# One iteration of a pipelined Mamba-2 block with a mixture of experts: the same operations in another order on every engine

## The reference

```python
# attention half (a Mamba-2 block), for each sequence
qkv = layernorm(x) @ W_in.T;  q = rope(qkv[:, :, 0])
zxbcdt = rmsnorm(q, norm_pre_w) @ W_zxbcdt.T              # z, (x, B, C), dt
xBC = silu(conv4(xBC) + conv_b);  dt = softplus(dt + dt_bias)
y = ssd(x_ssm, dt, -exp(A_log), B, C) + D * x_ssm         # scan over the sequence in chunks
out = rmsnorm(y * silu(z), norm_gated_w) @ W_out.T + q
x = x + layernorm(out)
# feed-forward half, for each token
h = layernorm(x)
shared = (silu(h @ sg.T) * (h @ su.T)) @ sd.T             # 512 hidden
scores = sigmoid(h @ router_w.T)                          # 16 experts in 4 groups
# the best 2 groups, the best 4 experts in them, their scores normalised: combine (token, expert)
routed = sum_e (silu(h @ gate_w[e]) * (h @ up_w[e]) * combine[:, e]) @ down_w[e]   # 16 x 64 hidden
x = x + layernorm(shared + routed)
```

## Time and profile before

| | us |
|---|---|
| median of 3 runs | 3214.55 (3213.54 to 3217.93) |
| the profiled execution | 3218.34 |
| its span | 3216.4 |
| TensorE, VectorE, ScalarE, POOL busy | 3116.9, 2393.1, 1931.1, 2033.7 |
| from one loop iteration to the next | 96.40 |

### The profile page before, as it was taken

How to read it: one execution, slowest core, us unless ns; L and a number is a source line. 1 busy time by engine, 2 the same in 40 slices (tenths; PEclk the granted TensorE clock), 3 DMA queues, 4 the chain that set the end, 5 groups by cost and what they waited for, 6 DMA issues and landing times.

```text
span 3216.4 us, 62379 instructions
## 1 busy us (share of the span) xinstructions
PE 3116.9 (97%) x19648; PEld 2723.4 (85%) x19648; DVE 2393.1 (74%) x5104; ACT 1931.1 (60%) x4146; POOL 2033.7 (63%) x2311
## 2 busy tenths in 40 slices
...
GB/s 109 40 70 80 66 59 74 73 76 79 66 60 75 72 77 78 66 60 74 72 78 76 66 63 72 72 79 76 66 65 71 71 79 76 66 67 69 71 80 40
DMA packets 143434, 227.33 MB, mean 71 GB/s; under 512 B 18977, under 2 KB 88353, under 8 KB 143393
## 3 DMA queue, kind: packets, MB, share of 16 engines
...
...
## 4 chain that ended last, share of the span: by engine, by line
PE 94%; POOL 1%; DMA 0%; DVE 0%; ACT 0%; issue 0%; SPq 0%; POOLq 0%; ACTq 0%; DVEq 0%
PE fpb L1325 33%; PE apb L1325 19%; PE acc L1504 17%; PE apb L1450 7%; PE apb L1334 4%; PE ppb L1325 3%; PE apb L1435 3%; PE apb L1442 2%; PE ppb L1344 2%; PE apb L1422 1%; PE fpb L1374 1%; PE fpb L1344 1%; PE fpb L1376 1%; PE fpb L1483 0%; PE apb L1395 0%; POOL hid L541 0%
## 5 line engine op out<-in xcount | busy, mean ns | idle before, releaser
L546 POOL TENSOR_TENSOR hidL<-hid,hidH 128x512 fp32r<-128x512 f32 x384 | 545.8, 1421 | 216.8 <-ACT hidH L801 207.5
L1015 DVE SCALAR_TENSOR_TENSOR xc<-apb,cw,xc 128x511 f32<-128x511 f32 (+2 forms) x576 | 427.8, 748 | 67.8 <-ACT xc L714 39.5
L1504 PE MATMUL acc<-WDH,hidH 128*128 128x256 f32 x1536 | 458.2, 298 | 6.2 <-POOLq L548 5.9
L801 ACT CAST hidH<-hid 128x512 fp32r<-128x512 f32 x384 | 236.1, 615 | 353.6 <-POOL hid L541 288.7
L1504 PE MATMUL acc<-WDH,hidL 128*128 128x256 f32 x1536 | 432.0, 281 | 0.0
L1504 PE MATMUL acc<-WDL,hidH 128*128 128x256 f32 x1536 | 431.5, 281 | 0.0
L541 POOL TENSOR_TENSOR hid<-hid,cb 128x512 f32<-128x512 f32 x256 | 347.2, 1356 | 81.8 <-DVEq L1136 43.7
L1134 DVE TENSOR_TENSOR hid<-hid,fpb 128x512 f32<-128x512 f32 x384 | 261.1, 680 | 135.4 <-PE fpb L1325 125.2
L1325 PE MATMUL fpb<-fTh,UH 128*128 128x512 f32 x768 | 336.1, 438 | 0.8 <-ACTq L793 0.8
L732 ACT ACTIVATE seg<-seg,acs 128x128 f32<-128x128 f32 x1024 | 313.8, 389 | 10.2 <-ACT cb L782 5.9
L1325 PE MATMUL fpb<-fTh,GH 128*128 128x512 f32 x768 | 317.5, 413 | 0.0
...
## 6 DMA issues: line engine op xcount, KB each, us to landing
seg<-acs_row SPq DMA_DIRECT2D x128, 512.0 KB, 4.2
cb<-c_row SPq DMA_DIRECT2D x512, 128.0 KB, 2.9
...
```

What stands on the lines that cost most here:

```text
L546: own.do(G.tensor_tensor(hidL[:, j % 2, :], hid[:, j % 2, :], hidH[:, j % 2, :].bitcast(fp32), ALU.subtract))
L801: A.copy(hidH[:, j % 2, :], hid[:, j % 2, :]).then_inc(sem["hidden_high"], 1)
L1015: ins = V.scalar_tensor_tensor(xc[:, b, s:], src[:, 0:T - s], cw[:, b, TAPS - 1 - s:TAPS - s], xc[:, b, s:], ALU.mult, ALU.add)
L1504: ins = nc.tensor.matmul(dst, l[:, w, tk], r[:, j, :], start=j == 0 and t % 2 == 0 and n == 0, stop=j == HB - 1 and n == 2, skip_group_che ...
```

## The change

Only orders change: the slots of A and F, FREED to match, and the five functions `iteration`. No operation is added or taken away on TensorE, VectorE, POOL and SyncE. On ScalarE `exp_table` and `silu_table` stand more often in the list. The diff of the five orders, without their indentation; the slots and FREED ("..." at its head) follow from them:

```diff
...
@@ -434,15 +434,14 @@  # SyncE
             def iteration(i, p, a, f, g):
 if f: save_x1(i - 1)
 if a: decay_store(); decay_rows(0); decay_rows(1)
+if p: load_next(i + 1)
 if f: combine_store(); combine_rows(0)
-if p: load_next(i + 1)
+if a: decay_rows(2)
 if f: combine_rows(1)
-if a: decay_rows(2); decay_rows(3)
+if a: decay_rows(3)
 if f: combine_rows(2)
-if a: keep_q()
-if f: combine_rows(3)
-if a: load_x(i)
-if f: combine_rows(4); combine_rows(5); combine_rows(6); combine_rows(7)
+if a: keep_q(); load_x(i)
+if f: combine_rows(3); combine_rows(4); combine_rows(5); combine_rows(6); combine_rows(7)
 if p: settle_p()
 if a: settle_a()
 if f: settle_f()
@@ -587,21 +586,20 @@  # POOL
 
             def iteration(i, p, a, f, g):
 if g: norm_out()
-if f: rest(0)
+if f: rest(0); rest(1)
+if a: mask(0)
 if g: add_result(i - 2)
-if f: rest(1); rest(2)
-if a: mask(0)
-if f: hold_shift()
-if a: mask(1)
+if f: rest(2)
 if g: result_stored()
-if a: decayed(0); decayed(1)
-if f: rest(3); combine(4)
-if a: gated(0)
-if f: combine(5); rest(4)
+if a: decayed(0); mask(1)
+if f: rest(3)
+if a: decayed(1); gated(0)
+if f: combine(4)
 if a: mask(2); decayed(2)
-if f: rest(5)
+if f: rest(4); combine(5)
 if p: norm_px()
-if a: mask(3); gated(1)
+if f: rest(5); hold_shift()
+if a: gated(1); mask(3)
 if f: combine(6)
 if a: gated(2)
 if f: rest(6)
@@ -609,16 +607,15 @@  # POOL, further down
 if f: combine(7)
 if p: rope_sum(0)
 if f: rest(7)
-if a: norm_mixed(0)
+if p: root_q(0)
 if f: combine(8)
-if a: gated(3)
+if a: norm_mixed(0); gated(3)
 if f: rest(8)
-if p: root_q(0)
+if p: rope_sum(1)
+if a: root_y(1)
 if f: combine(9)
-if a: root_y(1)
-if p: rope_sum(1)
+if p: root_q(1)
 if f: rest(9)
-if p: root_q(1)
 if a: norm_mixed(1); norm_x1(0)
 if f: combine(10)
 if a: norm_x1(1)
@@ -825,69 +822,63 @@  # ScalarE
 for names in freed.values():
     names.clear()
 if w: silu_table()
-if a: conv_first(4); silu_z(0, 0); silu_z(1, 0)
+if a: conv_first(4); silu_z(0, 0); silu_z(0, 1)
 if f: f_high(0); f_high(1)
-if a: conv_first(5); conv_silu(4); silu_z(2, 0); conv_silu(5); exp_table(); softplus()
-if a: conv_first(0); silu_table(); silu_z(3, 0)
+if a: conv_silu(4); silu_z(1, 0); silu_z(2, 0); exp_table(); softplus(); conv_first(5)
+if a: silu_table(); silu_z(3, 0); conv_first(0)
 if f: gate(0)
+if a: conv_silu(5)
+if f: gate(1)
 if a: conv_first(1); conv_silu(0)
-if f: score_tanh()
-if a: conv_first(2)
-if f: round_hidden(0)
-if a: conv_silu(1)
-if f: gate(1)
-if a: silu_z(0, 1); conv_silu(2)
-if f: gate(2)
 if g: final_norm()
-if a: conv_first(3)
-if f: round_hidden(1)
-if a: silu_z(1, 1)
+if a: conv_silu(1); conv_first(2)
+if f: round_hidden(0); round_hidden(1)
+if a: conv_first(3); conv_silu(2)
+if f: gate(2); score_tanh()
+if a: evac_B(); conv_silu(3); evac_CB(); exp_table(); decays()
 if f: round_hidden(2)
-if a: evac_B(); conv_silu(3)
-if f: gate(3); gate(4)
-if a: evac_CB(); silu_z(2, 1); exp_table(); decays()
-if f: evac_cT()
 if a: exp_seg(0)
 if w: split_high(3)
-if f: round_hidden(3)
-if a: exp_seg(1)
+if a: silu_table(); silu_z(1, 1); silu_z(2, 1)
+if f: gate(3)
+if a: silu_z(3, 1)
 if w: split_high(4)
+if f: gate(4); evac_cT(); round_hidden(3)
+if a: exp_table(); exp_seg(1)
+if w: split_high(5)
 if a: silu_table()
-if f: gate(5)
-if a: silu_z(3, 1)
-if w: split_high(5)
-if f: round_hidden(4); round_hidden(5); gate(6)
+if f: gate(5); round_hidden(4)
 if a: exp_table(); exp_seg(2)
 if w: split_high(6)
+if a: silu_table()
+if f: gate(6); round_hidden(5)
 if a: evac_y(0)
 if w: split_high(7)
-if p: norm_x(0)
-if a: exp_seg(3)
+if a: square_y(0)
 if w: split_high(8)
-if a: silu_table()
 if f: gate(7)
-if a: square_y(0)
+if p: norm_x(0); norm_x(1)
+if a: exp_table(); exp_seg(3)
 if w: split_high(9)
 if p: evac_xT(0)
+if f: round_hidden(6)
 if a: evac_y(1)
 if w: split_high(10)
-if f: round_hidden(6)
 if a: square_y(1)
 if w: split_high(11)
-if f: round_hidden(7); gate(8)
-if p: norm_x(1); square_q(0)
+if a: silu_table()
+if f: gate(8); round_hidden(7)
+if p: square_q(0); evac_xT(1)
 if a: evac_y(2)
-if p: evac_xT(1)
+if f: round_hidden(8)
 if a: square_y(2)
-if f: round_hidden(8); gate(9)
+if f: gate(9)
 if a: evac_y(3); square_y(3)
-if f: round_hidden(9)
 if p: square_q(1)
-if f: gate(10)
+if f: gate(10); round_hidden(9)
 if p: h_high(0); h_high(1)
-if f: gate(11)
 if a: norm_x1(0)
-if f: round_hidden(10)
+if f: gate(11); round_hidden(10)
 if a: norm_x1(1)
 if f: round_hidden(11)
 if p: settle_p()
@@ -1208,35 +1199,37 @@  # VectorE
             def iteration(p, a, f, g, w=False):
 for names in freed.values():
     names.clear()
-if a: dt_bias_add(0); dt_bias_add(1); conv(4)
+if a: dt_bias_add(0); conv(4); dt_bias_add(1)
 if f: f_low(0)
 if a: dt_bias_add(2)
 if f: f_low(1)
-if a: conv(5)
-if f: route_logits()
 if a: dt_bias_add(3)
 if g: final_moments()
-if a: dt_finish(); conv(0)
+if a: conv(5); dt_finish(); conv(0); conv(1)
 if f: up(0)
-if a: conv(1); conv(2)
-if f: route_scores()
 if a: evac_acs()
-if f: up(1); route_groups(); up(2)
+if f: up(1)
+if a: conv(2)
+if f: route_logits()
 if a: conv(3)
-if f: route_experts(); up(3)
-if a: times_dt(0); times_dt(1); decay_CB(0)
+if f: route_scores(); up(2); route_groups()
+if a: times_dt(0)
+if f: route_experts()
+if a: decay_CB(0)
+if f: up(3)
+if a: times_dt(1); chunk_y(0); new_state(0); decay_CB(1)
+if w: split_low(3)
 if f: up(4)
-if a: new_state(0); chunk_y(0)
+if a: times_dt(2)
 if f: up(5)
-if a: state_part(1); decay_CB(1)
-if w: split_low(3)
-if a: new_state(1); times_dt(2); chunk_y(1)
+if a: state_part(1)
+if p: moments_px()
+if a: new_state(1); chunk_y(1)
 if w: split_low(4)
-if p: moments_px()
+if a: decay_CB(2); state_part(2); y_low(0); new_state(2)
+if w: split_low(5)
 if f: up(6)
-if a: state_part(2); decay_CB(2); y_low(0); new_state(2)
-if w: split_low(5)
-if a: chunk_y(2); times_dt(3); decay_CB(3)
+if a: times_dt(3); chunk_y(2); decay_CB(3)
 if p: x_low(0)
 if a: y_low(1)
 if f: up(7)
@@ -1245,17 +1238,16 @@  # VectorE, further down
 if w: split_low(6); split_low(7)
 if a: state_part(3)
 if f: up(8)
-if a: chunk_y(3); y_low(2)
 if p: x_low(1)
-if a: add_x(0)
+if a: chunk_y(3); y_low(2); add_x(0)
 if w: split_low(8); split_low(9)
+if p: rope(1); norm_q(0)
+if a: y_low(3)
 if f: up(9)
-if a: y_low(3)
-if p: rope(1); norm_q(0)
 if a: mixed_out(1)
 if w: split_low(10)
+if p: norm_q(1); h_low(0)
 if f: up(10)
-if p: norm_q(1); h_low(0)
 if a: add_x(1)
 if w: split_low(11)
 if p: h_low(1)
@@ -1524,80 +1516,90 @@  # TensorE
 open_.update(n for n, (who, part, _, _) in SEM.items()
              if who == "PE" and {"p": p, "a": a, "f": f, "g": g}[part])
 if w: weights_split(KD + 1)
-if a: project_z(0, 0); project_z(1, 0)
+if a: project_z(0, 0)
 if f: ffn_by_channel(0)
+if a: project_z(0, 1)
+if f: ffn_by_channel(1)
 if a: project_x(4)
-if f: ffn_by_channel(1)
+if f: settled("ffn_in_ready")
 if g: down(10)
-if f: settled("ffn_in_ready")
-if a: project_z(2, 0); project_x(5)
+if a: project_z(1, 0); project_z(2, 0)
 if g: down(11); settled("last_split")
-if f: logits(0); logits(1)
-if a: project_z(3, 0); project_x(0)
+if a: project_z(3, 0); project_x(5)
 if f: gate(0)
+if a: project_x(0)
+if f: gate(1)
 if a: project_x(1)
 if f: up(0)
-if a: project_x(2)
-if f: gate(1); up(1)
-if a: project_z(0, 1); cumulate()
+if a: cumulate()
+if f: up(1)
+if a: settled("ad_ready"); project_x(2)
+if f: logits(0)
+if a: project_x(3)
+if f: logits(1)
+if a: CB()
 if f: gate(2)
-if a: settled("ad_ready"); project_z(1, 1); project_x(3)
+if a: B_by_token()
 if f: up(2); gate(3); down(0); settled("acc_free")
-if a: B_by_token(); project_z(2, 1)
-if f: gate(4)
-if a: CB(); x_by_token(0)
-if f: up(3); down(1)
-if a: x_by_token(1)
-if f: combine_by_expert(); down(2); settled("c_ready"); up(4); gate(5)
-if a: state(0); project_z(3, 1); diagonal(0)
+if a: x_by_token(0); project_z(1, 1)
+if f: down(1)
+if a: project_z(2, 1)
+if f: down(2)
+if a: project_z(3, 1)
+if f: gate(4); up(3)
+if a: state(0)
+if f: combine_by_expert()
+if a: x_by_token(1); diagonal(0)
+if f: up(4); settled("c_ready"); gate(5)
+if a: x_by_token(2)
+if f: down(3)
+if a: from_state(1); state(1)
 if f: up(5)
-if a: from_state(1); state(1)
-if f: down(3)
-if a: x_by_token(2)
+if a: diagonal(1)
 if f: gate(6)
-if a: diagonal(1); from_state(2)
-if f: up(6); down(4)
 if a: y_by_channel(0)
-if f: gate(7)
-if a: state(2)
-if f: up(7)
-if a: settled("xdec_ready"); diagonal(2); x_by_token(3)
+if f: gate(7); down(4)
+if a: from_state(2); state(2)
+if f: up(6)
+if a: settled("xdec_ready")
 if f: down(5)
+if a: x_by_token(3); diagonal(2)
+if f: gate(8)
 if a: settled("a_out_ACT")
 if w: weights_split(KD + 2)
 if a: project_out(0)
 if p: x_by_channel(0)
 if a: y_by_channel(1)
-if f: gate(8)
+if f: up(7)
 if a: from_state(3)
 if p: project_q(0)
 if a: project_out(1)
 if f: down(6); up(8)
-if a: y_by_channel(2); diagonal(3)
-if f: down(7)
-if a: settled("m_ready")
+if a: y_by_channel(2)
 if p: x_by_channel(1)
+if a: diagonal(3)
 if f: gate(9)
 if p: settled("xn_ready")
```

(39 more changed lines are left out.)

14 lines of the change are left out of this document (7 added, 7 removed).

## The result

The changed kernel takes 3242.32 us (median, 3240.67 to 3243.28), the kernel before beside it 3216.24: a ratio of 1.008, with 1.0062 to 1.0097 as its 95% interval. I had forecast 3212. It is slower by more than I could put down to a measurement.

The account below looks back on a forecast made before the run. TensorE was taken to bound the kernel. From the profiled 3218.34 us, -1.5 (boundary), +1 (ramp) and -2 (tail) gave 3215.8, and the median lying 3.8 lower gave 3212, no measurable change; range 3200 to 3240.

Parts of the forecast that it names:

- What bounds the kernel: Whole kernel: TensorE, busy 96.36 of a steady iteration's 96.40 us; only its lost time there can be won.
- the prize of the boundary: Between up(11) and the next project_z(0, 0): a wait of 0.28 us per iteration, 8.4 us or 0.26% over 30 boundaries.
- The boundary: From up(11) into the next iteration: h_low(1) early, the wait goes, new lateness takes 0.23; 96.35 us, a 1.5 us gain.
- the exchange with down(10): After the boundary: the 0.28 us won is mostly lost again, 0.19 at down(10) and 0.04 at the half z behind.
- The step that failed: Start of the iteration: project_z(0, 0) to down(10) keeps its length of 3.71 us in the new order.
- ScalarE: ScalarE's queue: ten table loads an iteration for six, 5.1 us more work, 65 of 96.4 us, covered; priced at 0.
- cover "in sum": ScalarE: four added loads cost nothing because its share only goes from 59.8 to 65 us of 96.4.
- Routing: Mid-iteration, route_experts to diagonal(0) and up(5): producers stay in time, slack 0.9 to 1.9 and 1.0 us; priced at 0.
- the slack of up(5): Mid-iteration: up(4) frees the bank at 47.8 and up(5) needs it at 48.8, slack 1.0 us.
- Rival B: Mid-iteration wait, route_experts through decay_CB and exp_seg(1) to up(5): 0.7 us an iteration, period 97.1, 3234 us; chance 0.27.
- Ramp (+1): Iteration 0: added loads nearly cancel with earlier CB and decays; +1 us, between -3 and +5.1.
- tail (-2): Last feed-forward: rests go ahead of the next combine, combine(11) starts about 2 us earlier; -2 us, between 0 and -3.

Follow-up runs that it names:

- before_hpair: Kernel before, TensorE's h_by_channel(0) ahead of up(10) and h_by_channel(1) ahead of gate(11), VectorE's h_low(0) and norm_q(1) ahead of up(10): 3218.08 us, ratio 0.9998.
- before_ffn1: Kernel before with one edit on TensorE, ffn_by_channel(1) ahead of project_x(4): 3237.44 us, ratio 1.0067.
- ffn_dve: Changed kernel with ffn_by_channel(1) back behind project_x(4) on TensorE and norm_q(0) behind y_low(3) and up(9) on VectorE: 3221.80 us, ratio 1.0012.
- dve_y: Changed kernel with norm_q(0) on VectorE moved behind y_low(3) but still ahead of up(9): 3229.60 us, ratio 1.0035.
- ffn_back: Changed kernel with ffn_by_channel(1) on TensorE moved back behind project_x(4): 3231.89 us, ratio 1.0042.
- dve_q: Changed kernel with norm_q(0) on VectorE moved behind y_low(3) and up(9): 3226.41 us, ratio 1.0027.
- no_loads: Changed kernel without its four added ScalarE table loads: 3240.70 us, ratio 1.007.
- before_loads: Kernel before with four more table loads an iteration, a pair behind exp_seg(0) and a pair behind exp_seg(2): 3285.68 us, ratio 1.0221.
- ffn_dve_loads: Changed kernel, ffn_by_channel(1) behind project_x(4), norm_q(0) behind y_low(3) and up(9), two more table loads in front of exp_seg(1): 3279.24 us, ratio 1.0198.
- before_h1: Kernel before with one edit on TensorE, h_by_channel(1) ahead of gate(11): 3237.75 us, ratio 1.0064.

## Why the prediction was wrong, by its own steps

- *What bounds the kernel: right.* TensorE, and the prize of the boundary is small. rest(10) and what follows up(11) give back what it wins (before_hpair).
- *The boundary: right in the size, wrong in the place.* h_low(1) is in time. Forecast were 0.28 won and 0.23 lost to down(10) and the half z behind it; before_hpair measured 0.23 and 0.22, and 96.36 for 96.35, which is closer than the two terms were. The changed kernel does win the 0.28: its boundary step is 0.24 in the mean and the one behind the first z matmul 0.12, for 0.44 and 0.20. But the exchange with down(10) never takes place there, since TensorE loses more before it gets to down(10).
- *The step that failed* is the sentence "project_z(0, 0) to down(10) is the same length in the new order (one half z, two ffn transposes, another half z, project_x(4): 3.71)". The length is the same, but the order inside it isn't. ffn_by_channel(1) went from 3.38 us after project_z(0, 0) to 1.89 (where it would start without a wait), and I never set it against its producer, though the prediction promises that for every block. So its wait was put at nothing without a reason. The row was there, in ScalarE's timeline of the kernel before (norm_x1(1); it ends 2.46 after the 1594.45 of the earlier trace rows):

```profile
1595.82 1.09 ACT L768 ACTIVATE xdt<-xc,nb,rstd 128x256 f32<-128x256 f32 x2
```

  That is 0.6 us too late for the new place, in the old order already; before_ffn1 shows that the hole takes nothing else. In the changed kernel the wait with its restart is 0.57 (project_z(0, 1) takes 1.36 us to the next block's start, 0.79 in ffn_dve).
- *A second term was missing.* On VectorE y_low(3) went behind rope(1) and norm_q(0). project_out(3) waits for it, 0.27 an iteration (dve_y), and more in iteration 0: there project_out(2) to project_out(3) takes 8.85 us in the changed kernel, 9.45 in ffn_back and 6.72 in dve_q and ffn_dve; it is 6.8 in the kernel before.
- *The period closes* to 0.07: 96.12 + 0.57 + 0.27 = 96.96, for 97.03 measured. ffn_dve, without both holes, wins 0.52 and not 0.84, since down(10) then waits 0.20 and the steps behind it take 0.12 more.
- *ScalarE: right.* Ten loads an iteration (the earlier trace rows after: x161 for x97 at each of the two places), 65.6 us busy, nothing lost in the loop (no_loads). My reason, cover "in sum", was too weak: before_loads has the same sum and loses 1.84. What decides is which activation stands behind the load, and what waits for that one.

```profile
L652 ACT ACT_TABLE_LOAD x161 | 206.6, 1283 | 4.4 <-POOL one L465 1.4 <-ACT hid L787 0.2
```

  Of the rule in the Trainium skill ("ScalarE: Activation LUTs", What ACT_TABLE_LOAD costs), a drain of about 1.38 us on top of each load, no run here shows any: the loads in a row stand 1.29 apart in ffn_dve_loads, the activation follows the last one's end by 0.02, and ahead of the 161 loads above ScalarE was idle for 4.4 us in all.
- *Routing: right.* In a steady iteration there is no wait at diagonal(0) or up(5); the slack of up(5) was 0.8 us by ffn_dve_loads (2.57 less 1.81), for 1.0 forecast. Rival B had the right sign and nearly the period (97.1; its time, 3234, is 8 us short) by luck, since its place was wrong: the kernel is slower through waits in the iteration, but for norm_x1(1) and y_low(3) and not for the routing.
- *Ramp (+1) and tail (-2): wrong, 4.3 and 3.1 measured.* Of the 4.3, 2.5 lie in iteration 0 and 2.1 in iteration 1 (98.95 us for 96.83), less 0.3 before. y_low(3)'s place has 2.1 of iteration 0. The rest can't be told from chance: the code of iteration 0 is the same in the kernel before, before_h1 and before_ffn1, which take 96.23, 94.31 and 96.60 us from its project_z(0, 0) to the next, and in the changed kernel and ffn_back, 98.74 and 96.47. Iteration 1 has the two holes too, which is 0.6 net; its other 1.5 was not tested. In the 3.1 are 0.6 of the last loop iteration, 0.8 of iteration 31 and 1.7 of the tail, where I had forecast a gain of 2. rest(10) holds the last down(10) as long as before:

```profile
3223.50 0.39 PE L1496 MATMUL acc<-WDH,hidH 128*128 128x256 f32 x1 [3.62 <-POOLq L547]
```

  The tail's 1.7 lie ahead of it: TensorE's waits for rest before a down grow by as much. The list of waits, in the window of the tail, before and after:

```profile
PE acc L1504 <- POOLq L548: 5.9, 5, 3.6
```

```profile
PE acc L1496 <- POOLq L547: 7.6, 7, 3.6
```

  So the new order of the hidden blocks made the rests late where I had them early; no run changed it in the tail alone.

- *What stays open.* ffn_dve has neither of the two holes and is still 0.12% over the kernel before: its period is 0.11 longer, with a wait of 0.20 at down(10) where the other has about as much at the boundary. The 0.11 seem to lie in steps of 0.08 at the first matmul behind a block of another kind, of which the new order has one or two more. That is read from the steps of one iteration and not tested.
